# A two-layer decoder on one core: layer 0's cross attention as one written-out stream of 32 row tiles, with separate PSUM banks for outputs and for the next sequence's projections

## What is computed

```
    def _L0_xattn_ref(q, k, v, mask, Wq, Wk, Wv, Wo):
        HEADS = 16
        D_MODEL = 256
        D_K = D_MODEL // HEADS
        b, s, _ = q.shape
        def proj(x, W):
            return (x @ W.T).reshape(b, -1, HEADS, D_K).transpose(0, 2, 1, 3)
        qh, kh, vh = (proj(q, Wq), proj(k, Wk), proj(v, Wv))
        att = jnp.einsum('bhqd,bhkd->bhqk', qh, kh) / jnp.sqrt(jnp.float32(D_K))
        att = jnp.where(mask, NEG, att)
        att = jax.nn.softmax(att, axis=-1)
        out = jnp.einsum('bhqk,bhkd->bhqd', att, vh)
        out = out.transpose(0, 2, 1, 3).reshape(b, -1, D_MODEL)
        return out @ Wo.T
```

## Time and profile before

| | us |
|---|---|
| median of three runs | 2730.04 |
| lowest and highest | 2725.38, 2740.86 |
| the profiled execution's own time | 2746.05 |
| its span, first to last instruction | 2744.1 |
| layer 0's cross attention, first to last instruction | 254.3 to 551.2 |
| its first tile's cap (L683) starts | 286.35 |

### The profile page before, as it was taken

One profiled execution on the slowest core, in us unless ns is written; L12 is line 12 of the kernel. 1 busy time (PEld: TensorE's weight loads), 2 busy tenths in 40 slices (PEclk: granted clock), 3 DMA queues, 4 the chain that ended last, 5 costly groups with the idle time before them and its releaser, 6 DMA issues. The chain is left out here.

```text
span 2744.1 us, 34995 instructions
## 1 busy us (share of the span) xinstructions
PE 2288.4 (83%) x10514; PEld 1595.4 (58%) x10515; DVE 1211.4 (44%) x3389; ACT 671.7 (24%) x1269; POOL 551.2 (20%) x748
## 2 busy tenths in 40 slices
PE   5887677760599984888888868988899999999998
PEld 3554344460377752555555536776577777777776
DVE  2442777662133335566666534554322222222234
ACT  1211233310011112444444432211122222222211
POOL 1110233217200013333333220011510000000043
PEclk9998899955799995799999989978899999999999
DMA  6000000042122223243333300005410101010033
GB/s 216 0 0 20 0 1 0 0 169 94 66 65 64 63 70 88 61 87 83 83 78 79 63 18 3 5 32 202 146 44 31 34 31 34 31 34 31 27 91 96
DMA packets 122392, 160.36 MB, mean 58 GB/s; under 512 B 21106, under 2 KB 90546, under 8 KB 122034
## 3 DMA queue, kind: packets, MB, share of 16 engines
q1 hardware_dynamic: 110002, 125.53, 16.3%
q0 software_dynamic: 12288, 33.57, 3.9%
HBM read 75.68 MB, written 49.28 MB: 46 GB/s over the span
## 5 line engine op out<-in xcount | busy, mean ns | idle before, releaser
L1437 PE MATMUL e_up_ps<-e_wgu,e_xT 128*128 x1152 | 344.9, 452 | 0.0
L1543 DVE TENSOR_TENSOR e_h<-e_act_g,e_up_ps 128x344 f32<-128x344 f32 x208 | 106.6, 513 | 492.5 <-PE e_ht_ps L1444 407.6
L2027 DVE CUSTOM_DVE_ANT_0 a_s_ps<-a_s_ps,a_causal 128x512 f32<-128x512 f32 (+3 forms) x512 | 241.1, 516 | 111.8 <-PE a_s_ps L1812 110.2
L1437 PEld LDWEIGHTS e_up_ps<-e_wgu,e_xT 128*128 128x128 f32 x1152 | 218.9, 190 | 103.7
L1951 ACT ACTIVATE a_prob<-a_st_ps 128x512 f32<-128x512 f32 (+1 forms) x384 | 197.6, 523 | 286.5 <-PE a_st_ps L1829 282.6
L1470 ACT ACTIVATE e_act_g<-e_up_ps 128x344 f32<-128x344 f32 x208 | 95.2, 458 | 695.5 <-DVE e_h L1543 406.3
L1812 PE MATMUL a_s_ps<-a_ks,a_qs 68*128 68x512 f32 (+3 forms) x512 | 154.5, 368 | 59.5 <-DVE a_most L2027 46.9
L1453 PE MATMUL e_y_ps<-e_wd,e_hT 128*128 x864 | 198.4, 379 | 0.0
L1829 PE MATMUL a_st_ps<-a_qs,a_ks 128*128 128x512 f32 (+3 forms) x512 | 184.7, 411 | 14.0 <-DMA a_qs<-a_m_lo 10.8
L1392 POOL DMA_INDIRECT e_wgu<-slots_y,slot x64 | 60.8, 950 | 661.6 <-DMA slots_y<-e_y 608.6
L1437 PE MATMUL e_up_ps<-e_own_gu,e_xT 128*128 128x344 f32 x512 | 164.3, 477 | 19.3 <-DVE e_xT L1483 13.8
(11 more groups left out here) (384 smaller groups left out, 3762.4 us busy)
## 6 DMA issues: line engine op xcount, KB each, us to landing
e_xin<-slots_x SPq DMA_DIRECT2D x144, 128.0 KB, 2.0
slots_y<-e_y SPq DMA_DIRECT2D x144, 128.0 KB, 1.7
slots_x<-zero_row SPq DMA_DIRECT2D x1, 9216.0 KB, 27.2
e_w<-in_L_ffn_w SPq DMA_DIRECT2D x16, 512.0 KB, 9.8
a_qs<-a_hi SPq DMA_DIRECT2D x32, 256.0 KB, 4.9
a_ks<-a_hi SPq DMA_DIRECT2D x32, 256.0 KB, 5.1
a_qs<-a_lo SPq DMA_DIRECT2D x32, 256.0 KB, 6.1
a_ks<-a_lo SPq DMA_DIRECT2D x32, 256.0 KB, 7.1
```

Of the source, the lines that this page charges most:

```text
L1437: last = pe.matmul(up_ps[:, 2 * half_ + u_, 0:H], xT[:, j, k * P:(k + 1) * P], up[:, k, u_, half_ * H:(half_ + 1) * H], start=k == 0, stop ...
L1543: dve.tensor_tensor(h[:, half_ * H:(half_ + 1) * H], act_g[:, :], up_ps[:, 2 * half_ + 1, 0:H], ALU.mult).then_inc(h_kept, 1)
L2027: last = dve.tensor_tensor_reduce(s_ps[:, u % 2, off:off + cols], s_ps[:, u % 2, off:off + cols], causal[:, S - cols:], 1.0, -3.0e38, ALU. ...
```

## The change

The stage now goes by single row tiles i = 0 to 31, in 37 steps that are written out without a loop. In step i each engine does the pieces of several tiles:

- TensorE: scores of tile i+1, turned probabilities of tile i-2, weighted values and projection of tile i-3.
- ScalarE: copy of the turned probabilities of i-2, copy of the weighted values of i-3, exponential of i.
- DVE: cap, maximum and subtraction of i, addition to x of i-4, sum and reciprocal of i-1.
- GpSimd: multiplication of i-1.

The next sequence is prepared at fixed places in the four steps of a sequence: transposes of its normed rows in the first (`turn_rows`, one half of the features at a time), its queries in the second (`query`, one half at a time), its values in the third; DVE takes the statistics of the sequence after in the third step, and copies the values and writes the normed rows in the fourth.

The PSUM banks are split anew: `seq_bank` (one bank) serves the next sequence's transposes, queries and values, one after the other; `out_bank` (one bank) holds one tile's weighted values in its first half (`o_half`) and its projected output in its second (`w_half`); `turn` holds only probabilities. `prob` is a ring of four tiles, `kblk` and `qT` are doubled, `probT` and `oT` hold two tiles.

What TensorE does, cut to its core:

```diff
+            def turn_rows(c, k):
+                pe.wait_ge(norm.rows_done, c * TB + TB)
+                if k == 0:
+                    after(pe, v_kept, c)
+                else:
+                    pe.wait_ge(norm.columns_done, c * KT + k)
+                for t in range(TB):
+                    last = pe.transpose(seq_bank[:, t * P:(t + 1) * P], norm.xn[:, t, k * P:(k + 1) * P], g.ident[:, :])
+                last.then_inc(norm.turned, 1)
...
+            def query(c, h):
+                pe.wait_ge(norm.columns_done, c * KT + KT)
+                if h:
+                    pe.wait_ge(q_kept, c * KT + h)
+                for k in range(KT):
+                    last = pe.matmul(seq_bank[:, :], wT[:, 0, k, h * P:(h + 1) * P], norm.xnT[:, k, :], start=k == 0, stop=k == KT - 1)
+                last.then_inc(q_done, 1)
...
+            def scores(i):
+                b = i // TB
+                pe.wait_ge(q_kept, b * KT + KT)
+                pe.wait_ge(kblk_done, b * KT + KT)
+                after(pe, capped, i - 1)
...
+            def turn_probs(i):
+                pe.wait_ge(prob_done, i + 1)
+                after(pe, p_kept, i)
...
+            def weighted(i):
+                pe.wait_ge(p_kept, i + 1)
+                pe.wait_ge(v_kept, i // TB + 1)
+                after(pe, x_done, i)
+                for n in range(PAIRS):
+                    r = 2 * HD * (n % 4)
+                    last = pe.matmul(o_half[r:r + 2 * HD, n // 4, :], vblk[:, i // TB % 2, n, :], probT[:, i % 2, n, :], start=True, stop=True)
+                last.then_inc(o_done, 1)
...
+            for i in range(STEPS):
+                if tile(i + 1):
+                    scores(i + 1)
+                if tile(i - 2):
+                    turn_probs(i - 2)
+                if next_sequence(i, 0):
+                    turn_rows(next_sequence(i, 0), 0)
+                if next_sequence(i, 1):
+                    query(next_sequence(i, 1), 0)
+                if next_sequence(i, 2):
+                    value(next_sequence(i, 2))
+                if tile(i - 3):
+                    weighted(i - 3)
+                if next_sequence(i, 0):
+                    turn_rows(next_sequence(i, 0), 1)
+                if next_sequence(i, 1):
+                    query(next_sequence(i, 1), 1)
+                if tile(i - 3):
+                    project_out(i - 3)
```

The loops of the other engines:

```diff
+            for i in range(STEPS):
+                if tile(i - 2):
+                    keep_turned(i - 2)
+                if next_sequence(i, 0):
+                    keep_columns(next_sequence(i, 0), 0)
+                if next_sequence(i, 1):
+                    keep_query(next_sequence(i, 1), 0)
+                if tile(i - 3):
+                    keep_weighted(i - 3)
+                if next_sequence(i, 0):
+                    keep_columns(next_sequence(i, 0), 1)
+                if next_sequence(i, 1):
+                    keep_query(next_sequence(i, 1), 1)
+                if tile(i):
+                    exponentials(i)
...
+            keep_value(0)
+            norm.vector_stats(1)
+            norm.vector_rows(1)
+            for i in range(STEPS):
+                if tile(i):
+                    masked(i)
+                if tile(i):
+                    maximum(i)
+                if tile(i - 4):
+                    add_to_x(i - 4)
+                if tile(i - 1):
+                    shares(i - 1)
+                if next_sequence(i, 2) and next_sequence(i, 2) + 1 < B:
+                    norm.vector_stats(next_sequence(i, 2) + 1)
+                if next_sequence(i, 3):
+                    keep_value(next_sequence(i, 3))
+                    if next_sequence(i, 3) + 1 < B:
+                        norm.vector_rows(next_sequence(i, 3) + 1)
...
+            for i in range(STEPS):
+                if tile(i - 1):
+                    normalise(i - 1)
+                if next_sequence(i, 0):
+                    blocks(next_sequence(i, 0))
+                if next_sequence(i, 1):
+                    both_halves(next_sequence(i, 1))
+                if next_sequence(i, 2) and next_sequence(i, 2) + 1 < B:
+                    norm.gpsimd(next_sequence(i, 2) + 1)
```

More of the change, by code:

```diff
@@ L120, in vector_rows @@
         v.wait_ge(self.rstd_done, b + 1)
-        after(v, self.turned, b - self.depth + 1)
+        after(v, self.turned, (b - self.depth + 1) * self.pieces)
         for s, n in free:
@@ L455, in l0_cross_attention @@
         head_of_key = sb("head_of_key", [P, 2 * HD])
-        kblk = sb("kblk", [P, KT, HH, SC])
+        kblk = sb("kblk", [P, 2, KT, HH, SC])
         ctx2 = sb("ctx2", [P, KT, 2, SC])
[L458 to L463, removed]
+        vblk = sb("vblk", [P, 2, PAIRS, 2 * HD])
+        qT = sb("qT", [P, 2, KT, S])
+        prob = sb("prob", [P, RING, HEADS * SC])
+        most, total, share = (sb(n, [P, RING, HEADS]) for n in ("most", "total", "share"))
+        probT = sb("probT", [P, 2, PAIRS, P])
+        oT = sb("oT", [P, 2, KT, P])
         loaded, masks, ready, caps = sem("loaded"), sem("masks"), sem("ready"), sem("caps")
@@ L473, in l0_cross_attention, with next_sequence @@
         block = ctx.enter_context(nc.Block())
+        STEPS = NT + 5
+        tile = lambda i: 0 <= i < NT
+        heads = lambda i: prob[:, i % RING].rearrange("p (h j) -> p h j", h=HEADS)
+        def next_sequence(i, t):
+            return i // TB + 1 if i % TB == t and i < NT and i // TB + 1 < B else None
         @block.sync
@@ L507, in normalise @@
[L507 to L519, removed]
@@ L595, in body @@
[L595 to L601, removed]
-                if within(b + 2):
-                    norm.tensor(b + 2, free=[(p_kept, b * TB + TB)] if back else ())
-                if back:
-                    values(b, j)
-                    project_out(b)
-                if within(b + 2):
-                    project(b + 2)
@@ new lines, in query, with value @@
+            def query(c, h):
[5 more added lines that the diff above has]
+                last.then_inc(q_done, 1)
+            def value(c):
+                pe.wait_ge(ctx2_done, c * 2 + 2)
+                pe.wait_ge(q_kept, c * KT + KT)
+                for k in range(KT):
+                    last = pe.matmul(seq_bank[:, 0:D], ctx2[:, k].rearrange("p a j -> p (a j)"), wT[:, 2, k, :], start=k == 0, stop=k == KT - 1)
+                last.then_inc(v_done, 1)
@@ new lines, in _ @@
+            for k in range(KT):
+                turn_rows(0, k)
+            for h in range(KT):
+                query(0, h)
+            value(0)
+            pe.wait_ge(kt_kept, 1)
+            scores(0)
+            for i in range(STEPS):
[17 more added lines that the diff above has]
+                    project_out(i - 3)
@@ new lines, in _ @@
+            for k in range(KT):
+                keep_columns(0, k)
+            for h in range(KT):
+                keep_query(0, h)
+            for i in range(STEPS):
[13 more added lines that the diff above has]
+                    exponentials(i)
```

227 lines of the change are left out of this document (78 added, 149 removed).

## The result

The changed kernel takes 2714.83 us (median of 20 runs, 2702.08 to 2730.81) against 2730.87 (20 runs) of the kernel before: a ratio of 0.9933, 95% interval 0.9911 to 0.9954. By that interval it is 13 to 24 us faster; the two medians lie 16 us apart. The forecast was 36 us (2694). The time lies inside the stated range of 2680 to 2718, near its upper end, but the gain is about half of the forecast's.

What follows compares the result with a forecast made beforehand. It took DVE's work plus one round trip through shared banks and ScalarE's order as the bound. Start, eight sequences and end summed to a last addition at 515.2 instead of 551.2: 36 us gained, 2694 us, range 2680 to 2718.

Steps and rivals of the forecast that it cites:

- What bound the kernel before: Old stage in steady state: DVE's work plus one round trip through shared banks and ScalarE's order, period 32.9 us.
- DVE's work per tile: DVE's cap, maximum, subtraction, sum with reciprocal and addition to x: 5.33 us for a step with nothing else.
- GpSimd's collisions: DVE standing behind GpSimd once per sequence: subtraction 0.7 us, normed rows 1.5, small statistics 0.45.
- More contention in every step: Rival: GpSimd's multiplication meets DVE's subtraction in every step, 22 us come back, 2716 us; chance 11%.
- The start: Second sequence's statistics and rows ahead of the first cap: it comes at 293.0 instead of 286.35, 6.7 us lost.
- The first sequence: Steps of 3.6, 5.0, 10.8 and 8.1, 27.5 us; exponential about 3 late in the third, TensorE at low clock.
- The period of 28.1: DVE's four steps of a sequence, 5.33, 6.0, 8.3 and 8.5 us, against 32.9 us before.
- the rival on the low clock: TensorE at half clock in the query step: DVE waits 6 us in each of seven periods, 2736 us; chance 8%.
- the tightest place: Second step, both query halves ahead of its exponential, which ends at 15.35 us, just when DVE wants it.
- The third rival: Same as the rival on the low clock: 6 us a period, 42 us against the gain of 36; chance 8%.
- The end: Last tile alone from sum to addition: 8.7 us, 10.5 with part at the low clock, ending at 515.2.
- the eighth sequence: Four steps of 5.33 us, from 483.4 to 504.7.

Runs made afterwards that it cites:

- oldswap: The kernel before with ScalarE's fourth exponential of a sequence ahead of the two query copies: stage 294.2 us (before 297.8, 297.2), ratio to before 0.9995.
- filler: Changed kernel with four transposes of the next normed rows made seven times from the third sequence on: stage 261.6 us (changed 275.5), ratio to before 0.9872.
- rows: Changed kernel with DVE writing the next normed rows ahead of the addition to x and sum in each fourth step: stage 258.9 us, ratio to before 0.983.
- add_early: Changed kernel with DVE's addition to x ahead of the maximum in every step: stage 269.5 us against 275.5; whole time not compared.

## Why the prediction was wrong by half

- **What bound the kernel before**: right as far as `oldswap` goes: DVE's work and one round trip, not ScalarE's order.
- **DVE's work per tile**, 5.33: measured 5.40 in steps without extras (499.91, 505.31 and 510.71 are caps that follow one another). About 0.3 us per sequence.
- **GpSimd's collisions**: rows 1.5 forecast, 1.4 to 1.5 found. The small statistics 0.45, found 0.54. The subtraction 0.7, found 0.4: taken singly, GpSimd's two products start at 415.49 and 416.49, so only 0.55 us of the first was left when DVE came to the subtraction at 415.98. The second product then stood behind the subtraction in turn: it takes 2.02 us, the first 1.04. The pair takes 3.02 us instead of 2.04, its time beside an idle DVE in the kernel before.

```profile
413.63 1.90 POOL L522 TENSOR_TENSOR c_prob<-c_prob,c_share 128x1024 f32<-128x1024 f32 x1 [6.66 <-DVE c_share L722]
415.49 3.02 POOL L513 TENSOR_TENSOR c_kblk<-c_kT,c_head_of_row 128x512 f32<-128x512 f32 x2
```

- **More contention in every step** (the first rival, 2716): not found, though the measured time is close to its figure. The subtraction meets GpSimd in one step of four and takes 1.22 us in the others. That the range, made wide for contention, holds the result is luck.

- **The start**, 6.7 us lost: 7.5 found.
- **The first sequence**, 27.5 us: 24.9 found. The forecast had the exponential 3 us late in its third step; DVE doesn't wait there, and the step takes 7.8 us instead of 10.8.
- **The period of 28.1**: it is the kernel's period when the clock is full (27.98), so the sum of the steps was right.
- **The step that failed** is in the rival on the low clock: "by the times above TensorE now never waits longer than 1.5 us". By those times TensorE ends its work 6.2 us into the fourth step, 2.3 before the step's end; scores and transposes take it to 0.4 us into the next first step, the first half of the turned rows to about 1 us, and the weighted values start 4.0 us into it. That is a wait of 3 us, from the forecast's own numbers, and 3.26 was found. The wait on `out_bank` was entered as a time at which an instruction starts, and the idle time ahead of it was never subtracted. It costs nothing by itself, since TensorE has slack there. It costs by the clock: the next 6.5 us of TensorE's work run at a mean clock of 0.53, the query step, correctly named as the tightest place with no slack, has its transposes 2.8 us late, and DVE loses 0.9 to 2.3 us in the third step of each sequence. `filler` removes it and gets 13.9 us, as much as was missing in the stage.
- **The third rival** had this mechanism with a wrong place (the query step itself at the low clock) and so a wrong size: 6 us a period instead of up to 2.3.
- **The end**: 12.5 us from the end of the 32nd step to the last addition against 10.5.
- **Luck in the sum**: with the clock at full (`filler`) the stage gains 36.2 us, but the start, the eighth sequence and the end cost 0.7, 0.3 and 2.0 us more than forecast, while the first sequence costs 2.6 less and the later periods together 0.7 less. These errors cancel to 0.3.
- In the whole time, the stage's 22 us lie within the 13 to 24 measured.

A bank shared in halves is what makes the wait. TensorE could write the weighted values into their half before DVE has read the other half, if the wait stood at the projection. The Trainium skill (PSUM — Partial Sum Buffer, "PSUM bank collisions raise a hardware error") says that two different engines that touch the same bank and the same 32 partitions of it at once raise an error, also at disjoint columns, and that a colliding reader mostly gets wrong data. No run here shows it; that version wasn't tried for this reason.

## What to carry to other kernels

When a schedule is worked out, write down each engine's idle times as well as its starts: an idle time of some 3 us on TensorE that costs nothing by itself can halve the speed of what follows, and what follows may be the tight chain. Where no better order can be had, useless transposes in the gap are a cheap fix (24 of them per sequence made the stage 14 us shorter), and an edit that shortens the gap helps to tell whether the clock is the reason. In a stage bound by DVE, put its instructions with SBUF inputs where GpSimd has nothing to do, ahead of the instruction that starts GpSimd and not behind it; here that was worth 1.5 us in 28.

## What the hardware showed unasked

The same idle time of 2.82 us left the clock at full in three first steps and let it fall in two of the same run; in `rows`, 2.24 us had it fall in four of five. 3.26 to 3.48 us had it fall each time, and idle times of 0.64 and 0.96 us alone never. In `add_early` 1.71 us of idle time, twelve transposes and a second idle time of 0.8 to 0.96 us follow one another, and the clock fell in one of five such places. The length of one idle time alone thus doesn't foretell the clock, and what else does isn't shown here.

A DVE instruction with two SBUF inputs and GpSimd hold each other up both ways, by turns: of two GpSimd products queued one behind the other the first held the subtraction up by 0.4 us, and the subtraction held up the second, which went from 1.04 to 2.02 us.
